# Scattering layer 1's expert results by pair of token and choice, and pacing the adds

## The reference

```
logits = x @ w_router;  w_topk, sel = top_k(softmax(logits), 4)
valid = pos < CAP                               # pos: place of the pair in its expert, CAP = 128
buf   = zeros((32, CAP + 1, 256)).at[sorted_e, dest].set(x[tok])
y     = einsum(silu(einsum(buf, w_gate)) * einsum(buf, w_up), w_down)
out   = zeros((T, 256)).at[tok].add(y[sorted_e, min(pos, CAP - 1)] * (w_topk * valid)[:, None])
sh    = silu(x @ sw_gate) * (x @ sw_up) @ sw_down
out   = out + sigmoid(x @ w_shared_gate) * sh
```

## Time and profile before

| | us |
|---|---|
| median of three runs | 1801.31 (1800.06 to 1802.41) |
| the profiled execution | 1804.75 |
| its span, first to last instruction | 1802.7 |
| layer 1: expert loop, about | 715 to 799 |
| layer 1: shared part, about | 799 to 923 |
| PE busy over the span | 1430.4 (79%) |
| DVE, ACT, POOL busy | 1149.8, 754.5, 595.2 |

### The profile page before, as it was taken

The page is one execution under the profiler, slowest core; times in us unless marked ns, Lnnn a source line. Parts: engine busy times, 40 slices in busy tenths (PEclk is TensorE's granted clock), DMA queues, the critical chain, the costliest instruction groups (busy, mean ns, idle before and its releaser), DMA issues. The chain is left out here.

```text
span 1802.7 us, 30396 instructions
## 1 busy us (share of the span) xinstructions
PE 1430.4 (79%) x8275; PEld 909.8 (50%) x8291; DVE 1149.8 (64%) x2546; ACT 754.5 (42%) x2273; POOL 595.2 (33%) x576
## 2 busy tenths in 40 slices
PE   4999993567589588997779999876883699975994
PEld 2565651345444253763346666553651466653552
DVE  3788887788578775324448999844335688844224
ACT  2766663344420032320027777521320588831321
POOL 2111100778477214335611111013436101002662
PEclk9999997898899678998879999957997799966997
DMA  7000000000010120962210001212433100411224
GB/s 251 10 6 9 9 4 1 1 0 0 13 35 0 52 91 29 305 213 80 87 31 10 12 9 62 87 56 56 122 102 87 36 24 23 154 52 33 82 81 154
DMA packets 73877, 111.35 MB, mean 62 GB/s; under 512 B 10381, under 2 KB 53200, under 8 KB 73296
## 3 DMA queue, kind: packets, MB, share of 16 engines
q1 hardware_dynamic: 61520, 77.99, 13.1%
q0 software_dynamic: 12288, 32.53, 6.5%
HBM read 87.41 MB, written 24.12 MB: 62 GB/s over the span
## 5 line engine op out<-in xcount | busy, mean ns | idle before, releaser
L523 ACT ACTIVATE l0a_prob<-l0a_ps_s,l0a_neg_max 128x128 f32<-128x128 f32 x512 | 141.0, 422 | 77.8 <-DVE l0a_neg_max L398 77.8
L523 ACT ACTIVATE l2a_prob<-l2a_ps_s,l2a_neg_max 128x128 f32<-128x128 f32 x512 | 141.0, 425 | 55.4 <-DVE l2a_neg_max L398 55.4
L878 ACT ACTIVATE l3a_prob<-l3a_ps_s,l3a_neg_max 128x256 f32<-128x256 f32 x256 | 104.5, 482 | 30.6 <-DVE l3a_neg_max L801 29.2
L398 DVE TENSOR_REDUCE l0a_neg_max<-l0a_ps_s 128x4 f32<-128x512 f32 x128 | 81.9, 684 | 38.0 <-PE l0a_ps_s L616 37.9
L369 POOL TENSOR_TENSOR l2a_k_head<-l2a_kT,head_of_row 128x512 f32<-128x512 f32 x32 | 32.6, 1041 | 178.7 <-ACT l2a_kT L504 178.7
L398 DVE TENSOR_REDUCE l2a_neg_max<-l2a_ps_s 128x4 f32<-128x512 f32 x128 | 82.1, 683 | 13.5 <-PE l2a_ps_s L616 13.4
L801 DVE TENSOR_REDUCE l3a_neg_max<-l3a_ps_s 128x2 f32<-128x512 f32 x128 | 84.2, 682 | 8.3 <-PE l3a_ps_s L929 8.0
L178 POOL TENSOR_TENSOR ln_rstd<-ln_var_eps,minus_half 128x16 f32<-128x16 f32 x8 | 23.4, 2921 | 196.3 <-POOLq L149 130.4
L1515 PE MATMUL l1a_ps_y<-l1a_kv,l1a_tap 128*128 128x512 f32 x192 | 84.2, 601 | 3.7 <-POOL l1a_kv L1487 3.7
L406 DVE COPY l2a_probT<-l2a_ps_t 128x512 f32<-128x512 f32 x128 | 82.0, 682 | 4.7 <-PE l2a_ps_t L625 4.6
L406 DVE COPY l0a_probT<-l0a_ps_t 128x512 f32<-128x512 f32 x128 | 82.1, 684 | 3.2 <-PE l0a_ps_t L625 3.1
(11 more groups left out here) (453 smaller groups left out, 3645.8 us busy)
## 6 DMA issues: line engine op xcount, KB each, us to landing
l1f_w_gu<-in_l1f_w_gu SPq DMA_DIRECT2D x32, 352.0 KB
expert_results<-l2f_y_sb SPq DMA_DIRECT2D x48, 128.0 KB
l1f_w_d<-in_l1f_w_d SPq DMA_DIRECT2D x32, 176.0 KB
expert_results<-l1f_y_sb SPq DMA_DIRECT2D x32, 128.0 KB
l2f_w_gu_all<-in_l2f_w_gu SPq DMA_DIRECT2D x1, 4096.0 KB, 13.7
l3f_w_gu_all<-in_l3f_w_gu SPq DMA_DIRECT2D x1, 4096.0 KB, 15.2
l3f_got<-expert_results SPq DMA_DIRECT2D x16, 256.0 KB, 5.1
x_rows<-in_x SPq DMA_DIRECT2D x8, 256.0 KB, 4.7
```

Source lines behind the costliest of these rows:

```text
L398: dve.tensor_reduce(neg_max[:, j, :], ps_s[j][:, :].rearrange("p (r k) -> p r k", r=R), AX.X, ALU.max, negate=True).then_inc(max_done, 1)
L523: last = act.activation(prob[4 * c + j][:, r * P:r * P + P], ps_s[j][:, r * P:r * P + P], ACT.Exp, bias=neg_max[:, j, r:r + 1])
L878: last = act.activation(prob[4 * c + j][:, m * D:m * D + D], ps_s[j][:, m * D:m * D + D], ACT.Exp, bias=neg_max[:, j, m:m + 1])
```

## The change

Layer 1 goes over to layer 3's way: `push` is true wherever there is a capacity. POOL scatters each expert tile's results in the loop, 7 tiles behind its gather, and SP reads 16 plain transfers of 512 KB afterwards, eight ahead. SP no longer stores in the loop. Since half of the pairs have no result, the rows that no scatter reaches must hold numbers: layer 0's feed-forward stage clears all 65 x 128 rows of `expert_results` with one transfer out of a zeroed tile, and the first scatter waits for it. The semaphores that two stages now share start from a count. In `got` the ring is 8 in layer 1. The pace of the adds goes from 640 to 768 columns per choice, in layers 1 and 2.

```diff
-MAX_SLOTS = 48 * P
+MAX_SLOTS = (4 * B + 1) * P
...
+        self.zeros = self.sb("zeros", [P, D], F32, self.early)
...
+        @block.sync
+        def _(sp):
+            sp.wait_ge(zeroed, 1)
+            sp.dma_start(core.results[:, :].rearrange("(n p) d -> p n d", p=P),
+                         core.zeros[:, :].unsqueeze(1).broadcast_to([P, 4 * B + 1, D])).then_inc(core.cleared, 16)
...
             all_rstd(pool, core, rstd_done)
+            pool.memset(core.zeros[:, :], 0.0).then_inc(zeroed, 1)
             pool.memset(ones[:, :], 1.0).then_inc(const_done, 1)
...
-    push = final
-    NG = GOT if push else RING
+    push = final or bool(capacity)
+    NG = GOT if push or capacity else RING
...
+            if capacity:
+                over_ring(sp, load, NT, RING, 2)
+                load_down(NT - 1, (NT - 1) % RING)
             if push:
                 for r in range(RING):
-                    sp.wait_ge(y_out[r], NT // RING * 16)
+                    sp.wait_ge(y_out[r], NT // RING * 16 + y_before[r])
...
-                    if t >= NG:
+                    if final and t >= NG:
                         sp.dma_start(core.out[t - NG], core.xt(t - NG)).then_inc(core.x_out, 16)
...
                 if j == 0:
                     pool.wait_ge(to_done, 1)
+                    pool.wait_ge(core.cleared, 16)
...
                 if after(j, RING):
-                    dve.wait_ge(y_out[r], (j - r) * (16 // RING))
+                    dve.wait_ge(y_out[r], (j - r) * (16 // RING) + y_before[r])
...
-                add_results(max(with_results, min(B, columns // (K * 640) - 1)))
+                add_results(max(with_results, min(B, columns // (K * 768) - 1)))
```

More of the change, by code:

```diff
@@ L109, in __init__ @@
         self.xin_in = [ctx.enter_context(nc.semaphore(f"xin_in{r}")) for r in range(RING)]
-        self.gathered = [ctx.enter_context(nc.semaphore(f"gathered{r}")) for r in range(RING)]
+        self.gathered = [ctx.enter_context(nc.semaphore(f"gathered{r}")) for r in range(GOT)]
         self.result_out = [ctx.enter_context(nc.semaphore(f"result_out{r}")) for r in range(RING)]
-        self.n_xin_in, self.n_gathered = 0, 0
+        self.n_xin_in, self.n_gathered = 0, [0] * GOT
+        self.n_result_out = 0
+        self.cleared = ctx.enter_context(nc.semaphore("results_cleared"))
         self.conv_in = ctx.enter_context(nc.semaphore("conv_in"))
@@ L1057, in hadamard_ffn @@
         rstd_done = sem("rstd_done")
+        zeroed = sem("zeroed")
         block = st.enter_context(nc.Block())
+        @block.sync
[3 more added lines that the diff above has]
+                         core.zeros[:, :].unsqueeze(1).broadcast_to([P, 4 * B + 1, D])).then_inc(core.cleared, 16)
         @block.gpsimd
@@ L1668, in moe_ffn @@
         y_out = [sem(f"y_out{r}") for r in range(RING)]
-        xin_in, got_in = core.xin_in, core.gathered
+        xin_in = core.xin_in
+        y_before = [0] * RING
         if push:
-            got_in, y_out = [sem(f"got_in{r}") for r in range(NG)], core.result_out
-        xin_before, got_before = core.n_xin_in, core.n_gathered
+            y_out, y_before = core.result_out, [core.n_result_out] * RING
+            core.n_result_out += NT // RING * 16
+        xin_before, got_before = core.n_xin_in, tuple(core.n_gathered)
         core.n_xin_in += NT // RING * 16
-        core.n_gathered += B // RING * K * 16
+        got_in = [sem(f"got_in{r}") for r in range(NG)] if push else core.gathered[0:NG]
+        if not push:
+            for r in range(NG):
+                core.n_gathered[r] += B // NG * K * 16
         n_loads = 1 + rms + biased
@@ L1822, in _ @@
             for t in range(B):
-                if t >= RING:
-                    pool.wait_ge(added, t - (RING - 1))
+                if t >= NG:
+                    pool.wait_ge(added, t - (NG - 1))
                 for k in range(K):
                     pool.indirect_dma_start(
-                        out=got[t % RING][:, k, :], out_offset=None, in_=results,
+                        out=got[t % NG][:, k, :], out_offset=None, in_=results,
                         in_offset=bass.IndirectOffsetOnAxis(ap=from_slot[:, t, k:k + 1], axis=0))\
-                        .then_inc(got_in[t % RING], 16)
+                        .then_inc(got_in[t % NG], 16)
         @block.vector
@@ L2072, in add_results @@
                 for t in range(with_results, until):
-                    dve.wait_ge(got_in[t % NG], (t // NG + 1) * 16 if push else got_before + (t // NG + 1) * 16 * K)
+                    dve.wait_ge(got_in[t % NG], (t // NG + 1) * 16 if push else got_before[t % NG] + (t // NG + 1) * 16 * K)
                     for k in range(K):
```

## The result

The changed kernel takes 1791.39 us, the median of five runs (1788.38 to 1793.64), beside 1801.54 us of the kernel before. The ratio is 0.9943, with a 95% interval of 0.9929 to 0.9956: 0.6% faster, 10 us. Forecast were 1775.6 us and a range of 1768 to 1794. The sign was right, but the gain is 10.2 us where the sum said 25.7. The time lies in the range, but outside the likeliest case's 1770 to 1781: it falls in the part of the range that was kept for half of rival B.

A forecast was written before the change was run, and what follows sets the result against it. PE was taken as the bound, DMA a close second (97.4% in the expert loop). The terms -32.1 + 4.9 + 1.5 = -25.7 took the profiled 1804.75 to 1779.1, as a median 1775.6 us; range 1768 to 1794.

The forecast's parts named there:

- The sign: Whole kernel: the change makes it faster, chance 0.86; within 0.2% (3.6 us) the same 0.03, slower 0.11.
- rival B: Layer 1's expert loop: back-to-back issues by POOL bring the holds there, 15 to 23 us back, about 1795 us; chance 0.13.
- Gathers go: Layer 1's shared part: without POOL's 64 gathers all holds and the slow clock vanish, -32.1 us; bounds -32.1 to 0.
- hold: Layer 1's shared part: ACT or DVE waits with unnamed releaser though PE's output was ready; three of 13.4, 9.5, 4.4 us.
- The pace: End of layer 1: later pacing leaves two blocks of adds after PE's end, +4.9 us; bounds +4.5 to +5.5.
- The results come by plain transfers: Layer 1's shared part: SP's plain transfers land in time for DVE's adds, costing nothing; bounds 0 to 2 us.
- Scatters join the loop: Layer 1's expert loop: scatters make POOL slightly slower than PE and bytes change queue, +1.5 us; bounds -1 to 6.4.
- Layer 2: Layer 2's tail: the pace keeps tile 3 back, taken as 0; +2.5 if a stall stays, -3 if a hold goes.
- Outside layer 1: Layer 0: clearing 8.5 MB runs beside compute and costs 0; +2 us if a code load waits behind it.
- A: Rival, layer 1's shared part: holds are instruction waits and stay, so the kernel is slower, 1807.7 us; chance 0.10.
- C: Rival: layer 1's expert loop stretches to its bound of 6.4 us and layer 2 by 2.5, 1783 us; chance 0.14.
- D: Rival, layer 1's shared part: clock not fully granted or products late, some 10 of 32 us stay, 1786 us; chance 0.08.

The follow-up runs named there:

- e8c_before_short_pause: The kernel before plus a 0.55 us POOL memset behind every second gather of the tails, on chip 5: 1793.42 us, ratio 0.9943.
- b0_before: The kernel before the change, unchanged, profiled on chip 2: 1772.15 us, ratio 0.9996.
- v1_two_of_three: The changed kernel with 19 y tiles in layer 1 and two scatters per three tiles from tile 9, the rest behind, chip 15: 1776.83 us, ratio 1.0020.
- v2_pace: v1_two_of_three with layer 1's adds paced by 640 columns and layer 2's by 768, on chip 15: 1771.60 us, ratio 1.0000.
- e6_before_paused: The kernel before plus a POOL drain and memset behind every second gather of layers 1 and 2's tails, on chip 0: 1883.29 us, ratio 1.0426.
- e1_sp_stores: The changed kernel with layer 1's loop results leaving by SP's plain stores instead of POOL's scatters, on chip 0: 1781.24 us, ratio 0.9862.
- a0_after: The changed kernel, unchanged, on chip 2: 1778.66 us, ratio 1.0031.
- e3_pace_640: The changed kernel with adds paced by 640 columns per choice again instead of 768, on chip 15: 1771.34 us, ratio 0.9989.
- e2_empty_scatters: The changed kernel with every row number of layer 1's scatters out of bounds, so they write nothing, on chip 0: 1797.72 us, ratio 0.9955.
- e8b_before_short_pause: The kernel before plus a 0.55 us POOL memset behind every second gather of the tails, on chip 2: 1788.83 us, ratio 1.0093.

## Why the prediction was right in part and wrong in size

- **"Gathers go", -32.1, with the pace 4.9: right.** Forecast -27.2 for the stretch, measured -27.83. For the cause there was only a coincidence, and it was counted too well: ACT's first hold and one of DVE end while POOL gathers on, so it holds for three of five. e8c_before_short_pause now shows that the gathers' row without pauses is the cause (the same 64 gathers, no hold, and 8 us less than the kernel before on the same chip), and b0_before the size, 29.95 us. PE's part is 92.43 us there and 89.63 after, so 2.8 of the 32.7 us that PE's part lost are not holds.
- **"The pace", +4.9: right.** In layer 1 v1_two_of_three takes 95.75 us and v2_pace 90.83, 4.92 less. PE's part (89.6) is 0.7 us under the 90.3 worked out.
- **"The results come by plain transfers", nothing: right.** SP's first transfer is issued at 818.68, 3.2 us behind the start of the shared part, no add waits for one, and each lands in 4.1 us.
- **"Scatters join the loop", +1.5: this step failed.** It came to +15.95. The working counted what POOL, the y ring and the DMA queues have to do, and by these it was right: on chip 2, where nothing is held, the step measures +1.88. The other 14.07 us are holds, and the sum had put them at nothing. It left out the very mechanism that the step before it had just removed 32.1 us for. If POOL's back-to-back issues hold the signals in the tail, they do so in the loop, where the change puts 60 of them, mostly 0.30 us apart. Rival B said this, with 15 to 23 us and 1795 us, and it happened: 14.5 us over the forecast of the step, 1791.4 us, in waits of 3.7 us at most and not in two or three of 7.8. I gave it 0.13 because layer 3's loop shows no holds. But there POOL stands idle for 1.03 us before the scatter of a pair, and e8c_before_short_pause shows that a pause of 0.55 us already takes the holds from a row of gathers. Nor is layer 3's loop safe: in e6_before_paused, on chip 0, it has a hold of 2.33 us behind six issues 0.30 us apart (1757.56 to 1765.07). The argument against B was an argument for it.
- **"Layer 2", 0: inside its bounds, but close to the lower one.** It measured -2.78. The pace costs about 2 us (476.6 against 474.5 in the means above; +2.19 on chip 2, within the bound of +2.5). The kernel before loses a few us there to holds, 478.29 against 475.54 in b0_before, and the changed kernel has no remote wait there (the bound of -3). Each is of the size by which traces of the same pace differ.
- **"Outside layer 1", 0:** right for layer 0. The last stretch is 1.56 us longer here and equal on chip 2; its scatter over all traces is 1.7 us.
- **A, C and D** did not happen. e1_sp_stores rules out A's reason (instruction fetches) for the loop: nearly the same code of ACT, DVE and PE runs there without a hold.
- **The sign** was right by the luck of the chip. On chip 2 the same two kernels differ by +0.3%, the other way, since there are no holds to remove. No row of the prediction could tell this, and none of its rivals says it.

The sum on a chip without holds is +4.9 - 2.8 (PE's part, 92.43 in b0_before and 89.6 after) + 1.88 + 2.19 = +6.2, which is the measured difference of the spans.

## What to carry to other kernels

When a stall is explained by what one engine does, ask of every step that moves this work whether it does the same in its new place, and price it there by the same rows. Here some of the holds went with the indirect DMAs from the tail into the loop: 30 us were removed in the one and 14 paid in the other. And where a profile has waits of several us whose releaser it can't name, run the unchanged kernel on other chips before tuning for them: on chip 2 this change costs 0.3%, in the first runs it gave 0.6%, and without holds the pace alone (768 or 640 columns) makes 0.4%, from 1.0031 (1.0019 to 1.0042) in a0_after to 0.9989 (0.9977 to 1.0001) in e3_pace_640.

## What the runs showed of the hardware that I had not expected

- The holds go with the chip. The kernel before takes 1801 to 1804 us in the first runs and on chips 0 and 5, and 1772 to 1773 us on chips 15 and 2, and the same each time on chips 2 and 5, which were used twice. With the same program, POOL's instructions take the same time on both (a gather 0.95 us every 1.25); what comes late is the start of ACT and DVE after PE's product. None of the ten traces from chips 15 and 2 has a wait marked remote. In the changed kernel and with empty scatters POOL's own waits for PE are marked remote too, up to 0.9 and 1.4 us. What in a chip makes the difference is not shown.
- They need no data: with scatters whose every row is out of bounds ACT still has 14.7 us of waits marked remote (e2_empty_scatters). The Trainium skill ("SBUF — State Buffer", SBUF: two separate sides) says that of the compute engines only VectorE and GpSimd can block each other, through a shared port pair, and that a DMA issued by GpSimd can be late because an instruction of VectorE has that pair. The trace does not fit this rule: the indirect DMAs' own length does not change, and ACT, which the rule leaves out, has the longest hold, 13.41 us.
- `drain` on POOL behind an indirect DMA takes 2 us (e6_before_paused). A memset of 0.55 us in the same place starts at once (e8b_before_short_pause: a gather ends at 827.65 + 0.94, the memset starts at 828.59).
- The gathers themselves are no slower on a chip with holds: the last of layer 1 starts at 897.6 and 896.2 us in the two runs of the paused kernel on chips without holds, at 898.4 us on chip 5.
